# Landmark attention stage of a six-stage decoder kernel: four separate turns rewritten as one list of steps, and one small triangular inverse moved to VectorE

## The chip, the cores and the metric

One core of a Trainium2 chip runs one program. The metric is the device time of that program in microseconds (us), where the result holds for one launch over all four batches.

## What is computed

Two decoder layers with a LayerNorm behind each residual: delta rule, Mamba-like scan, sign FFN, landmark attention, cross attention, ternary FFN, on x of 4 x 512 x 512 in float32. The change is in the fourth (landmark) and has one small part in the first (delta).

```python
q, k, v = split(x @ w_qkv + b_qkv)                    # 32 heads of 16
q, k = rope(q), rope(k)                               # pairs of channels rotated by position
out_local = masked_softmax(q kT / 4, causal) v        # in blocks of 64 tokens
lmf = pool(k, v)                                      # softmax(pool_q k) v: 4 landmarks a block, 32 in all
lmf += attention(lmf @ w_lm_qkv) @ w_lm_out + b       # landmark to landmark
lmf += softmax((lmf @ w_l2t_q + b) k) v @ w_l2t_out + b   # landmarks read their tokens
gk, gv = split(lmf @ w_lm_kv + b)
out_global = masked_softmax(q gkT / 4, earlier blocks) gv
gate = sigmoid(x @ w_gate + b_gate)
y = ((1 - gate) * out_local + gate * out_global) @ w_out + b_out
```

In the delta stage the inverse of a unit lower triangular 32 x 32 matrix is needed for each chunk of 32 tokens and head; the kernel takes half a batch's heads at a time (eight such pairs, n = 0 to 7): 128 matrices stand side by side, one a partition, and are inverted in 31 columns.

## The kernel before

The program is a chain of stages (`STAGES`), each of which waits until the one before has stored all of its output. Each engine has its own instruction list. A stage with `unrolled` has one list over all four batches; the landmark stage has not: each engine runs a loop of four turns, one per batch (`sp_turn`, `pool_turn`, `pe_turn`, `act_turn`, `dve_turn`). PSUM's eight banks are a ring (`Ring`): each product has its place in the plan, and TensorE waits until the bank's former content is read.

A turn has these parts.

- **Front.** x is turned over on TensorE (L204) and copied by ScalarE (L213), the gate is projected (L237), then v, and for each of four token tiles q and k (L224, one projection is four float32 matmuls of 512 columns, and each float32 matmul is two records in the trace). VectorE adds the bias and rotates q and k token by token (L2478 to L2488), TensorE turns them over (L2212), ScalarE copies them to QT and KT (L2307). v is copied by 16 small DMAs into the zero-padded VV (L2034).
- **Local.** 16 items (channel chunk c, token tile t). GpSimd multiplies a block of KT with a head mask into Kz (L2049, two buffers, `landmark_kz`), TensorE makes the scores (L2234), VectorE adds the mask (L2575), takes the maximum (L2383), subtracts it (L2385), ScalarE takes exp (L2346), VectorE sums (L2495), TensorE transposes (L2241), ScalarE copies (L2351), TensorE multiplies with VV (L2252), ScalarE copies the result (L2355). The order is in `local_order`: scores of item i+2, transposes of i, values of i-1. Into each step one step of the landmark chain (`CHAIN`, 15 steps: pool, landmark attention, reading, global keys and values) is put. The normalization is left to the end: GpSimd multiplies the four output tiles with (1 - gate)/sum (L2055).
- **Global.** Eight items (token tile, half of the heads) with the landmarks' keys: scores (L2264), mask, maximum, subtract (L2634, L2383, L2385), exp, sum (L2605), transposes (L2271), values (L2278, token-major), then `mix`: scale by gate/sum and add to the local part (L2612 to L2624).
- **Out.** The mixed output is turned over (L2286), multiplied with w_out (L224), residual and bias are added (L2648, L2650), and the tiles are normalized and stored.

The stage's matrices (12 of 512 x 512 float32, 1 MB each) are loaded once at its begin and stay.

In the delta stage GpSimd does all eight inverses (L535 to L547, `pool_all`): a copy of the identity, and for each of 31 columns a product (L541) and a subtraction (L543), each waiting for the one before. SyncE cuts the matrices out through DRAM (L496, L500) and brings the inverse back through DRAM (L511, L515, `sp_inverse`); TensorE's triangles of that pair (L622, `pe_triangles`) wait for it. PSUM's ring has six banks there; VectorE's reads of V (L996, `dve_beta_v`) and of PT (L1005) release them.

Of the kernel before, what the change touches and what calls it, by code (L numbers as in the profile page):

```python
# [342 lines left out]
class Delta(Stage):  # L343
# [561 lines left out]

    def dve_all(self, dve):
        s = self
        for p in range(-1, s.PAIRS + 1):
# [972 lines left out]
class Landmark(Stage):  # L1881
# [3 lines left out]
    name, pool_works = "landmark", True  # L1885
# [4 lines left out]
    EPS = 1e-9  # L1890

    CHAIN_BANKS = {
        "pool_s": [(("pool", "s"), "dve")], "pool_T": [(("pool", "T"), "act")],
        "pool_v": [(("pool", 0), "dve"), (("pool", 1), "dve")],
        "lqk": [(("lq", "rows"), "dve"), ("lq", "dve"), (("lk", "rows"), "dve"), ("lk", "dve")], "lv": [("lv", "dve")],
        "ls": [(("ls", 0), "dve"), (("ls", 1), "dve")], "lpT": [("lpT", "act")], "lo": [("lo", "dve")],
        "loT": [("loT", "act")], "lout": [(("lout", "rows"), "dve"), ("lout", "dve")], "l2q": [(("l2q", "rows"), "dve"), ("l2q", "dve")],
        "read_s": [(("read", "s"), "dve")], "read_T": [(("read", "T"), "act")],
        "read_v": [(("read", 0), "dve"), (("read", 1), "dve")],
        "rout": [(("rout", "rows"), "dve"), ("rout", "dve")], "gkv": [(("gk", "rows"), "dve"), ("gk", "dve"), ("gv", "dve")],  # L1900
    }
    CHAIN = list(CHAIN_BANKS)
    SMALL = ["lq", "lk", "lout", "l2q", "rout", "gk"]

    def __init__(self, io, carve, ps, x_in, x_out):
        s = self
        s.io, s.x_in, s.x_out = io, x_in, x_out
        s.wqkv, s.wlm = carve(C, 3 * D), carve(C, 3 * D)
        s.wlo, s.wl2q, s.wl2o, s.wkv, s.wo = carve(C, D), carve(C, D), carve(C, D), carve(C, 2 * D), carve(C, D)
        s.wg = carve(C, s.H)  # L1910
        s.bqkv, s.blv, s.bgv, s.bo, s.bg = carve(3 * D), carve(D), carve(D), carve(D), carve(s.H)
        s.blq, s.blk, s.blo, s.bl2q, s.bl2o, s.bgk = (carve(C) for _ in range(6))
# [4 lines left out]
        s.rope = carve(T, 6, 8)  # L1917

        tokens, turned, rotated = carve(T, D), carve(C, L), carve(T, D)
        s.x, s.xT, s.xr = tokens, turned, rotated  # L1920
        s.raw, s.rot = rotated[:, 0:2], rotated[:, 2:4]
        s.Kz = Arena(tokens.rearrange("p t n -> p (t n)"))(2, s.HC, P)
        a = Arena(turned.rearrange("p t n -> p (t n)"))
        s.kz, s.vz, s.lm4 = a(C, s.HC, s.NL), a(s.HC, 4, s.DH), a(C, 4, s.NL)
        a = Arena(rotated.rearrange("p t n -> p (t n)"))
        s.lp, s.l2z = a(2, D), a(C, s.NB, s.HC, s.M)

        s.cs, s.cT, s.cmx, s.rows = carve(2, D), carve(4, P), carve(s.H), carve(2, P)
        s.tmp = s.cT.rearrange("p a n -> p (a n)")
        s.v, s.QT, s.KT, s.lout = carve(T, D), carve(C, L), carve(C, L), carve(T, D)  # L1930
        s.VV = carve(s.NB, C, 2, s.S)
        s.sc, s.p, s.pT = carve(2, D), carve(2, D), carve(2, 4, P)
        s.gate, s.ungated, s.lsum, s.gsum = (carve(T, s.H) for _ in range(4))
        s.mx = carve(2, s.H)
# [3 lines left out]
        s.r, s.y = s.v, s.QT  # L1938

        s.items = [(c, t) for c in range(C) for t in range(T)]  # L1940
        plan = [(("xT", t), "act") for t in range(T)]
        plan += [("gateT", "dve"), (("v", 0), "dve"), ("gate", "dve")] + [(("v", t), "dve") for t in range(1, T)]
        for t in range(T):
            plan += [(("q", t), "dve"), (("k", t), "dve")]
            if t:
                plan += [(("qT", t - 1), "act"), (("kT", t - 1), "act")]
        plan += [(("qT", T - 1), "act"), (("kT", T - 1), "act")]
        for what, i in s.local_order():
            if what == "landmarks":
                plan += s.CHAIN_BANKS[i]  # L1950
            else:
                plan += [((what, i), {"s": "dve", "t": "act", "o": "act"}[what])]
        for what, i in s.global_order():
            plan += [((what, i), {"gs": "dve", "gt": "act", "go": "dve"}[what])]
        plan += [(("oT", t), "act") for t in range(T)] + [(("y", t), "dve") for t in range(T)]
        s.ring = Ring("landmark", ps, 0, 8, plan)

    def local_order(self):

        n, step = len(self.items), 0
        for i in range(-2, n + 1):
            if i + 2 < n:
                yield "s", i + 2
            if 0 <= i < n:
                yield "t", i
            if 0 <= i - 1 < n:
                yield "o", i - 1
            if i >= -1 and step < len(self.CHAIN):  # L1970
                yield "landmarks", self.CHAIN[step]
                step += 1

    def global_order(self):

        n = 2 * T
        for i in range(-2, n + 1):
            if i + 2 < n:
                yield "gs", i + 2
            if 0 <= i < n:  # L1980
                yield "gt", i
            if i > 0 and i % 2 == 0:
                yield "go", i // 2 - 1

    def sp_before(self, sp):
        s, io, w = self, self.io, "landmark_weights"
        sp.e.dma_start(s.ident, io["c_masks"][:, 0, :]).then_inc(*sp.up(w, 16))
        for dst, src in ((s.blq, "D_blq"), (s.blk, "D_blk"), (s.blo, "D_blo"), (s.bl2q, "D_bl2q"),
                         (s.bl2o, "D_bl2o"), (s.bgk, "D_bgk"), (s.pool, "D_pool")):
            sp.e.dma_start(dst, io[src]).then_inc(*sp.up(w, 16))  # L1990
        for dst, src in ((s.bm16, "c_group16"), (s.gm32, "c_group32"), (s.m_local, "c_local"),
                         (s.m_gl, "c_global"), (s.valid, "c_valid0"), (s.rope, "c_rope")):
            sp.e.dma_start(dst, io[src]).then_inc(*sp.up(w, 16))
        sp.e.dma_start(s.m_lm[:s.NL], io["c_landmark"]).then_inc(*sp.up(w, 16))
        for dst, src in ((s.bg, io["D_bg"]), (s.bqkv, io["D_bqkv"])):
            sp.e.dma_start(dst, src.partition_broadcast(P)).then_inc(*sp.up(w, 16))
# [16 lines left out]
    def act_before(self, act):  # L2013
        act.e.wait_ge(*act.at_all("landmark_weights"))
# [1631 lines left out]
```

## Time and profile before

| | us |
|---|---|
| median of three runs | 3797.43 (3789.03 to 3804.51) |
| the profiled execution: its time | 3791.86 |
| its span, first to last instruction | 3790.1 |
| TensorE busy | 2899.1 (76%) |
| VectorE busy | 2316.3 (61%) |
| ScalarE busy | 1230.9 (32%) |
| GpSimd busy | 1104.9 (29%) |

Times in the trace count from the span's start. The landmark stage takes 1931.4 to 2855.6. A busy TensorE is not one at its peak: its records overlap, and the granted clock (1.00 is 2.4 GHz, 0.50 is 1.2 GHz) differs between stretches. Idle time of an engine that nobody waits for costs nothing.

### The profile page before, as it was taken

How to read it: one execution, taken by the hardware profiler on the slowest of the kernel's cores; microseconds unless marked ns; L12 is line 12 of the kernel's file. 1: busy time of each engine (PE TensorE's matmuls, PEld its weight loads, DVE VectorE, ACT ScalarE, POOL GpSimd, SP SyncE). 2: the span in 40 equal slices, each digit the busy share in tenths (PEclk: the TensorE clock that was granted, in tenths of full speed). 3: DMA queues.
4: the chain of work that ended last, by engine and by line, in shares of the span. 5: the costliest groups of instructions: out<-in, count | busy, mean ns of one | idle time of the engine just before them, and what ended most of it. 6: DMA issues, size and time to landing. Idle time of an engine off the chain costs nothing.

```text
span 3790.1 us, 53260 instructions
## 1 busy us (share of the span) xinstructions
PE 2899.1 (76%) x20710; PEld 1511.5 (40%) x20710; DVE 2316.3 (61%) x3434; ACT 1230.9 (32%) x2016; POOL 1104.9 (29%) x1044
## 2 busy tenths in 40 slices
PE   6688888755555655599968787888874798989877
PEld 4565655522121212244434545455452233333233
DVE  1233333338898989687728668585763565656577
ACT  3232323214434333111102212121221464645645
POOL 4433333325454645200003012020203442433000
PEclk8788998867777778899988888888876899999999
DMA  2212121112212020400050000000004543434211
GB/s 76 67 45 66 45 66 45 43 42 106 81 37 89 22 90 11 173 23 38 27 202 1 24 23 24 23 13 29 6 12 117 104 108 71 105 73 87 82 45 45
DMA packets 194861, 226.12 MB, mean 60 GB/s; under 512 B 98520, under 2 KB 130808, under 8 KB 193712
## 3 DMA queue, kind: packets, MB, share of 16 engines
q1 hardware_dynamic: 193520, 218.44, 20.5%
q0 software_dynamic: 1088, 4.19, 0.3%
q8 instruction: 172, 2.82, 0.3%
q14 instruction: 81, 0.66, 0.1%
HBM read 154.69 MB, written 54.92 MB: 55 GB/s over the span
## 4 chain that ended last, share of the span: by engine, by line
PE 38%; DVE 12%; issue 6%; ACT 3%; DMA 2%; POOL 1%; SPq 1%; DVEq 0%; ACTq 0%; POOLq 0%
PE ps L224 6%; PE ps L1723 4%; PE ps L1734 4%; PE ps L3001 3%; PE ps L2988 3%; PE ps L2976 2%; PE ps L2937 2%; PE ps L2967 2%; DVE arena L2383 1%; PE ps L2234 1%; PE ps L2278 1%; PE ps L2099 1%; DVE arena L1333 1%; PE ps L2252 1%; ACT arena L3079 1%
## 5 line engine op out<-in xcount | busy, mean ns | idle before, releaser
L3174 DVE TENSOR_REDUCE arena<-ps 128x1 f32<-128x512 f32 x512 | 330.4, 685 | 272.4 <-PE ps L2976 271.1
L224 PE MATMUL ps<-arena 128*128 128x512 f32 (+3 forms) x1296 | 469.6, 519 | 10.5 <-ACT arena L855 3.3
L1381 PE MATMUL ps<-arena 128*128 128x512 f32 x512 | 312.5, 755 | 130.0 <-POOL arena L1365 130.0
L1365 POOL TENSOR_TENSOR arena<-arena 128x1024 f32<-128x1024 f32 x128 | 309.5, 2418 | 298.7 <-DVE arena L1357 297.7
L3079 ACT ACTIVATE arena<-ps 128x512 f32<-128x512 f32 x512 | 288.0, 597 | 289.1 <-PE ps L2988 285.5
L1357 DVE TENSOR_TENSOR_SCAN arena<-ps,arena 128x1024 f32<-128x1024 f32 x128 | 291.6, 2278 | 63.6 <-ACT ps L1348 63.2
L2049 POOL TENSOR_TENSOR arena<-arena 128x1024 f32<-128x1024 f32 x64 | 127.7, 1999 | 598.0 <-ACT arena L2307 354.8
L224 PEld LDWEIGHTS ps<-arena 128*128 128x128 f32 (+2 forms) x1296 | 196.1, 155 | 250.6 <-issue 182.8
L541 POOL TENSOR_TENSOR arena<-arena 128x31 f32<-128x31 f32 (+15 forms) x248 | 150.0, 605 | 368.9 <-DMA arena<-d_a 350.1
L1348 ACT ACTIVATE ps<-arena 128x511 f32<-128x511 f32 x256 | 165.2, 680 | 241.2 <-DVE arena L1357 241.0
L1381 PEld LDWEIGHTS ps<-arena 128*128 128x128 f32 x512 | 114.8, 238 | 320.0 <-POOL arena L1365 190.0
L2988 PE MATMUL ps<-arena 99*128 99x512 bf16 x512 | 198.2, 390 | 55.1 <-ACT arena L3079 33.4
L2976 PE MATMUL ps<-arena 96*128 96x512 bf16 x512 | 197.9, 389 | 24.4 <-issue 18.9
L1723 PE MATMUL ps<-arena 128*128 128x512 bf16 x768 | 169.0, 382 | 8.0 <-issue 8.0
L1734 PE MATMUL ps<-arena 128*128 128x512 bf16 x768 | 166.9, 379 | 0.0
L1333 DVE TENSOR_TENSOR arena<-ps,arena 128x1024 f32<-128x1024 f32 x128 | 154.3, 1206 | 0.8
L1029 DVE TENSOR_TENSOR arena<-ps,arena 128x256 f32<-128x256 f32 x120 | 50.9, 425 | 158.9 <-PE ps L742 158.9
L3001 PE MATMUL ps<-arena 128*32 128x512 f32 x1024 | 141.6, 626 | 1.0 <-ACT arena L3079 1.0
L543 POOL TENSOR_TENSOR arena<-arena 128x31 f32<-128x31 f32 (+15 forms) x248 | 134.5, 542 | 19.4
L2874 POOL TENSOR_TENSOR arena<-arena 128x512 f32<-128x512 f32 x32 | 40.8, 1275 | 318.0 <-ACT arena L3052 318.0
L2988 PEld LDWEIGHTS ps<-arena 99*128 99x128 bf16 x512 | 49.7, 98 | 207.1 <-ACT arena L3079 143.1
L1377 PE MATMUL ps<-arena 128*128 128x512 f32 x32 | 32.3, 1111 | 116.1 <-DVE arena L1407 116.1
(337 smaller groups left out, 5394.9 us busy)
## 6 DMA issues: line engine op xcount, KB each, us to landing
arena<-d_bc SPq DMA_DIRECT2D x32, 1024.0 KB, 5.2
arena<-d_x SPq DMA_DIRECT2D x24, 1024.0 KB, 5.5
arena<-d_parts SPq DMA_DIRECT2D x192, 128.0 KB, 4.3
d_x<-arena SPq DMA_DIRECT2D x20, 1024.0 KB, 4.4
d_parts<-arena SPq DMA_DIRECT2D x32, 384.0 KB, 2.4
arena<-arena SPq DMA_DIRECT2D x64, 128.0 KB, 2.0
d_w<-arena SPq DMA_DIRECT2D x3, 1408.0 KB, 4.8
arena<-d_w SPq DMA_DIRECT2D x3, 1408.0 KB, 10.5
```

The costliest lines, as they stand in the source:

```text
L224: ins = pe.e.matmul(ps[:m, :n], lhsT(k), rhs(k), start=(k == 0), stop=(k == chunks - 1))
L1333: dve.e.tensor_tensor(s.h[:, i % s.HS].rearrange("p (w l) -> p w l", w=s.W), spread(s.ps[:, s.DTU, :], 1, s.W), s.bc[:, turn % s.SLOTS, 0] ...
L1357: dve.e.tensor_tensor_scan(h, s.dA[:, i % 2].rearrange("p w l -> p (w l)"), h, 0.0, ALU.mult, ALU.add).then_inc(*dve.up("scan_scanned"))
L1365: pool.e.tensor_tensor(h, h, s.bc[:, turn % s.SLOTS, 1], ALU.mult).then_inc(*pool.up("scan_hC"))
L1381: ins = pe.e.matmul(y, s.ident, s.h[:, i % s.HS, w * L:(w + 1) * L], start=False, stop=last)
L1723: ins = e.matmul(ps, s.up[:, k, m * P:(m + 1) * P], s.xp[i][:, k, :], start=(k == i == 0), stop=(k == C - 1 and i == 2))
L1734: ins = e.matmul(ps, s.hp[i][:, m, t * P:(t + 1) * P], s.down[:, m, :], start=(m == i == 0), stop=(m == s.FC - 1 and i == 2))
L2976: pe.e.matmul(s.rmax.bank((u, m)), s.Qs[:s.N, slot, h, t * P:(t + 1) * P], s.Ks[:s.N, slot, h, :], start=True, stop=True).then_inc(*s.rmax ...
L2988: pe.e.matmul(s.rexp.bank((u, i)), s.Ks[:s.N + 3, slot, s.G * g + j, k * P:(k + 1) * P], s.Qs[:s.N + 3, slot, s.G * g + j, :], start=True, ...
L3001: ins = e.matmul(ps[32 * j:32 * j + 32, :], s.V[:, u % s.SLOTS, k, s.G * g + j, :], s.E[:, k % 2, j, :], start=(k == 0), stop=(k == s.KEYS ...
L3079: act.e.activation(s.E[:, k % 2, j], s.rexp.bank((u, i)), ACT.Exp).then_inc(*s.rexp.empty(act, (u, i)))
L3174: dve.e.tensor_reduce(s.mx[:, u % 2, t, h:h + 1], s.rmax.bank((u, m)), AX.X, ALU.max, negate=True).then_inc(*s.rmax.empty(dve, (u, m)))
```

## The change

**Landmark.** The stage becomes `unrolled`: `schedule` yields one list of steps, and each engine walks it and does its share of each step. A batch is 20 local steps (k = -2 to 17), 11 global steps (k = -2 to 8) and 4 out steps. The front of batch b+1 is put into the steps of batch b: x, gate and v into local steps 0 to 7, and eight projections "r" (q and k of each of four channel chunks, already channel-major, so that they need not be turned over) into local steps 9, 10, 12, 13 and global steps -1, 1, 3, 5. Batch 0's front stands alone at the begin.

The rotation is now channel-major on GpSimd: ScalarE adds the bias on its copy from PSUM, two DMAs of SyncE's queue swap even and odd partitions, and GpSimd does three 128 x 512 operations.

```diff
+    def pool_rope(self, pool, b, r):
+        pool.e.wait_ge(*s.ring.at_emptied(pool, ("r", b, r)))
+        e.tensor_tensor(s.m1, s.raw[:, j % 2], s.cos, ALU.mult).then_inc(*pool.up("landmark_cos"))
...
+        pool.e.wait_ge(*pool.on("landmark_swapped", j))
+        e.tensor_tensor(s.sw[:, j % 2], s.sw[:, j % 2], s.sin, ALU.mult).then_inc(*pool.up("landmark_sin"))
...
+        e.tensor_tensor((s.QT, s.KT)[w][:, b % 2, c], s.m1, s.sw[:, j % 2], ALU.add).then_inc(*pool.up("landmark_rot"))
+    def sp_swap(self, sp, b, r):
+        sp.e.wait_ge(*s.ring.at_emptied(sp, ("r", b, r)))
...
+        for odd in range(2):
+            sp.e.dma_start(s.sw[odd::2, j % 2], s.raw[1 - odd::2, j % 2])
+        sp.e.wait_ge(*sp.on("landmark_swapped", j))
```

The softmax weights of the local and global items are normalized and gated before they are transposed, item by item: VectorE makes the factor, GpSimd multiplies. GpSimd's order in a local and a global step is this:

```diff
+            if phase == "local":
+                if s.item(k + 1) is not None:
+                    s.pool_scale(pool, b, k + 1)
+                if k == -2:
+                    s.pool_kz(pool, b, 0)
+                if s.item(k + 3) is not None:
+                    s.pool_kz(pool, b, k + 3)
+            if phase == "global" and s.item(k + 1, s.NG) is not None:
+                s.pool_g_scale(pool, b, k + 1)
+            for what, i in front:
+                if what == "r":
+                    s.pool_rope(pool, b + 1, i)
...
+            if phase == "global" and k >= s.NG - 3 and b + 1 < B:
+                for i in range(2):
+                    s.pool_pairs(pool, b + 1, 2 * (k - s.NG + 3) + i)
```

The other engines' order in a local step:

```diff
+    def pe_all(self, pe):
+            if phase == "local":
+                if s.item(k + 2) is not None:
+                    s.pe_scores(pe, b, k + 2)
+                if s.item(k) is not None:
+                    pe.e.wait_ge(*pe.on("landmark_scaled", b * s.N + k))
+                    s.pe_turn(pe, ("t", b, k), k)
+                if s.item(k - 1) is not None:
+                    s.pe_values(pe, b, k - 1)
...
+            if chain:
+                s.pe_landmarks(pe, chain, b)
+            for what, i in front:
+                s.pe_front(pe, what, b + 1, i)
+    def dve_all(self, dve):
+                if s.item(k + 2) is not None:
+                    s.dve_scores(dve, b, k + 2)
+                if s.item(k + 1) is not None:
+                    s.dve_factor(dve, b, k + 1)
+    def dve_factor(self, dve, b, i):
+        e.tensor_reduce(ls, s.p[:, i % 3].rearrange("p (h n) -> p h n", n=s.S), AX.X, ALU.add).then_inc(*dve.up_step(st))
...
+        e.scalar_tensor_tensor(ls, ls, s.EPS, s.rungated[:, b % 2, t, c * s.HC:(c + 1) * s.HC], ALU.max, ALU.mult).then_inc(*dve.up_step(st))
+        e.reciprocal(ls, ls).then_inc(*dve.up("landmark_factor"))
```

The value products come out channel-major: four local items fill one bank "o", and the global values are four products of 512 columns ("go", two at step 4 and two at step 8) added to it, so that the turning over before w_out (L2286), `mix` and GpSimd's scaling of the output (L2055) go. VV is now filled by four DMAs and eight GpSimd multiplications with a pair mask (`pool_pairs`). The bias b_out is added to x by GpSimd (local step 7), where VectorE did it before (L2650). The chain has 18 steps (lq, lk and gk, gv apart). Only w_q, w_k and w_gate stay; the ten matrices of the chain, v and w_out go through three slots of 1 MB and are loaded anew for each batch (`sp_matrix`).

**Delta.** GpSimd's loop begins at n = 1; the first inverse is done on VectorE by the same operations, put behind `dve_beta_k` of pair 0:

```diff
-        for n in range(s.PAIRS):
-            if n:
-                pool.e.wait_ge(*pool.on("delta_t32_out", n - 1))
+        for n in range(1, s.PAIRS):
+            pool.e.wait_ge(*pool.on("delta_t32_out", n - 1))
...
                     if i == 1:
                         s.dve_beta_k(dve, n)
+                        if n == 0:
+                            s.dve_inverse(dve)
```

## Rows read from the trace of the kernel before

**Rows 1.** Busy time by stretch: the stage's begin and one turn

```profile
1931.40:1954.60 23.20, 0.00 (x0) 0.00 (x0) 0.81 (x4) 0.00 (x0) 4.37 (x2) 0.50 0.78 287
...
2181.67:2404.80 223.13, 183.67 (x1591) 113.00 (x1595) 152.98 (x249) 48.69 (x93) 37.24 (x21) 0.84 0.07 21
```

Columns of rows 1 and 2: stretch, us; busy us (instructions) of TensorE, its weight loads, VectorE, ScalarE, GpSimd; granted clock; DMA share; GB/s.

**Rows 2.** The same view, one turn in its four parts

```profile
2181.67:2236.00 54.33, 48.49 (x161) 23.57 (x161) 30.05 (x46) 5.52 (x9) 3.78 (x2) 0.94 0.14 39
2236.00:2338.00 102.00, 84.32 (x1199) 53.09 (x1198) 80.28 (x126) 26.25 (x55) 28.16 (x14) 0.83 0.04 12
2338.00:2378.00 40.00, 28.30 (x146) 23.61 (x145) 30.26 (x53) 9.82 (x18) 5.29 (x5) 0.76 0.08 27
2378.00:2404.80 26.80, 22.56 (x90) 12.73 (x93) 12.40 (x25) 7.11 (x11) 0.00 (x0) 0.82 0.02 6
```

**Rows 3.** Groups by line in the turn 2181.67 to 2404.80

```profile
L2049 POOL TENSOR_TENSOR arena<-arena 128x1024 f32<-128x1024 f32 x16 | 31.9, 2002 | 158.7 <-ACT arena L2307 98.3 <-PE ps L2234 60.4
...
L2385 DVE TENSOR_TENSOR arena<-arena 128x512 f32<-128x512 f32 (+1 forms) x25 | 21.6, 864 | 0.9
L2383 DVE TENSOR_REDUCE arena<-arena 128x8 f32<-128x512 f32 (+2 forms) x25 | 17.7, 707 | 0.9
...
L2398 DVE RECIPROCAL arena<-arena 128x8 f32<-128x8 f32 x2 | 0.4, 203 | 0.1
```

**Rows 4.** GpSimd's scaling of a 128 x 512 tile: one line's instructions, ns min/median/max

```profile
L2055 POOL TENSOR_TENSOR arena<-arena x16: 1055/1058/1507, 2115.9 to 2789.7; 128x512 f32<-128x512 f32 x16
```

**Rows 5.** Timeline of the turn, TensorE: start, us, engine, line

```profile
2240.49 1.08 PE L2234 MATMUL ps<-arena 128*64 128x512 f32 x4
...
2241.50 0.66 PE L2241 MATMUL ps<-arena 128*128 128x128 f32 x4
...
2248.28 1.98 PE L2234 MATMUL ps<-arena 128*64 128x512 f32 x4
...
2260.05 0.91 PE L2252 MATMUL ps<-arena 128*64 128x32 f32 x16
```

**Rows 6.** Timeline, TensorE: seven projections, 56 records

```profile
2187.72 24.20 PE L224 MATMUL ps<-arena 128*128 128x512 f32 x56
```

**Rows 7.** Groups by line in the same turn: two steps of the chain

```profile
L2099 PE MATMUL ps<-arena 64*32 64x32 f32 (+1 forms) x488 | 9.2, 236 | 0.7 <-issue 0.7
...
L2143 PE MATMUL ps<-arena 32*128 32x32 f32 x16 | 3.6, 397 | 2.9 <-ACT arena L2324 2.9
```

**Rows 8.** The cross stage's like rotation: GpSimd's product, the swap's landing

```profile
L2874 POOL TENSOR_TENSOR arena<-arena x32: 1264/1276/1287, 2890.1 to 3470.1; 128x512 f32<-128x512 f32 x32
...
L2796 SPq DMA_DIRECT2D arena<-arena x64: 465/568/601, 2890.0 to 3468.4; - x64
...
DMA to landing us min/median/max: 1.9/2.0/5.5
```

**Rows 9.** Timeline: VectorE alone, and beside a GpSimd operation

```profile
2203.57 0.43 DVE L2486 TENSOR_TENSOR arena<-arena 128x256 f32<-128x256 f32 x1
...
2213.57 1.89 POOL L2049 TENSOR_TENSOR arena<-arena 128x1024 f32<-128x1024 f32 x1 [92.42 <-ACT arena L2307]
2213.59 2.16 DVE L2486 TENSOR_TENSOR arena<-arena 128x256 f32<-128x256 f32 x1
```

**Rows 10.** Timeline: from the turn's last product to its store

```profile
2398.19 0.69 DVE L2648 TENSOR_TENSOR arena<-arena,ps 128x512 f32<-128x512 f32 x1 [1.29 <-PE ps L224]
...
2403.54 0.40 SPq L311 DMA_DIRECT2D d_x<-arena  x1
```

**Rows 11.** Timeline of the delta stage's begin

```profile
60.03 0.26 POOL L541 TENSOR_TENSOR arena<-arena 128x31 f32<-128x31 f32 x1 [45.68 <-DMA arena<-d_a]
...
72.30 8.61 PE L605 MATMUL ps<-arena 128*128 128x256 f32 x32
...
101.64 0.27 POOL L543 TENSOR_TENSOR arena<-arena 128x31 f32<-128x31 f32 x1
...
110.14 3.21 PE L622 MATMUL ps<-arena 128*32 128x128 f32 x64 [29.24 <-DMA arena<-d_t]
```

More of the change, by code:

```diff
@@ L1881 @@
 class Landmark(Stage):
-    name, pool_works = "landmark", True
+    name, pool_works, unrolled = "landmark", True, True
     H, DH, M, S = 32, 16, 4, 64
@@ L1890 @@
     EPS = 1e-9
[L1892 to L1901, printed above, removed]
@@ L1937, in __init__ @@
         s.norm = Norm("landmark", carve)
[L1938 to L1983, printed above, removed]
+        s.steps = list(s.schedule())
+        s.ring = Ring("landmark", ps, 0, 7, [e for step in s.steps for e in s.entries(*step)])
+        s.ro = Ring("landmark_o", ps, 7, 1, [(("o", b, c), "act") for b in range(B) for c in range(C)])
@@ new lines, in __init__, with turns, schedule @@
+        s.uses = [(name, b, n) for n, step in enumerate(s.steps) for name, b in s.matrices(*step)]
+        s.use = {use[:2]: i for i, use in enumerate(s.uses)}
+    def turns(self, name):
+        s = self
+        if name in s.ONCE + s.RING:
+            return 1
+        return B * s.N if name in s.BY_ITEM else B * s.NG if name in s.BY_GLOBAL else B * len(s.TURNED) if name in s.BY_TURNED else B
+    def schedule(self):
+        s = self
+        nothing = {}
+        for fronts in (s.LOCAL_FRONT, s.GLOBAL_FRONT):
+            for k in fronts:
+                yield "front", -1, k, None, fronts[k]
+        for b in range(B):
+            more = b + 1 < B
+            for k in range(-2, s.N + 2):
+                yield "local", b, k, s.CHAIN[k + 1] if 0 <= k + 1 < len(s.CHAIN) else None, (s.LOCAL_FRONT if more else nothing).get(k, [])
+            for k in range(-2, s.NG + 1):
+                yield "global", b, k, None, (s.GLOBAL_FRONT if more else nothing).get(k, [])
+            for t in range(T):
+                yield "out", b, t, None, []
@@ L1994, in sp_before @@
[L1994 to L2002 removed]
+        s.loaded = 0
@@ new lines, in act_sqrt, with act_all @@
+    def act_sqrt(self, act, b):
+        act.b = b
+        self.norm.act_sqrt(act)
+        act.b = 0
+    def act_all(self, act):
+        s = self
+        for phase, b, k, chain, front in s.steps:
+            if phase == "local":
+                if k == -2 and b:
+                    s.act_sqrt(act, b - 1)
+                if s.item(k) is not None:
+                    s.act_turned(act, b, k)
+                if k >= 1 and (k - 1) % T == T - 1:
+                    s.act_out(act, b, (k - 1) // T)
+            if phase == "global":
+                s.act_global(act, b, k)
+            if chain:
+                s.act_landmarks(act, chain, b)
+            for what, i in front:
+                s.act_front(act, what, b + 1, i)
+            if phase == "local" and s.item(k + 2) is not None:
+                s.act_exp(act, b, k + 2)
+        s.act_sqrt(act, B - 1)
@@ new lines, in dve_scale @@
+    def dve_scale(self, dve, b):
+        dve.b = b
+        self.norm.dve_scale(dve, self.x, self.x)
+        dve.b = 0
+    def dve_all(self, dve):
+        s = self
+        dve.e.wait_ge(*dve.at_all("landmark_late"))
+        for phase, b, k, chain, front in s.steps:
+            if phase == "local":
+                if k == -2 and b:
+                    s.dve_scale(dve, b - 1)
+                if s.item(k + 2) is not None:
+                    s.dve_scores(dve, b, k + 2)
+                if s.item(k + 1) is not None:
+                    s.dve_factor(dve, b, k + 1)
+            if phase == "global":
+                s.dve_global(dve, b, k)
+            if phase == "out":
+                s.dve_y(dve, b, k)
+            if chain in ("pool_T", "read_T"):
+                s.dve_pool_weights(dve, chain, b)
+            if chain:
+                s.dve_landmarks(dve, chain, b)
+            for what, i in front:
+                s.dve_front(dve, what, b + 1, i)
+            if chain in s.SMALL:
+                s.dve_small(dve, chain, b)
+        s.dve_scale(dve, B - 1)
```

1260 lines of the change are left out of this document (688 added, 572 removed).

## The prediction

> **What bounds the kernel now.** I read first the busy time by stretch. The landmark stage is a head of 23.2 us without matmuls and four like turns of 223.1 us, in which TensorE is busy for 184, VectorE for 153 and GpSimd for only 37 us [rows 1]. By parts, a turn spends 54.3 us on the front, 102.0 on local, 40.0 on global and 26.8 on the output [rows 2]; in none is one engine busy all the time, so each part is bound by the hand-overs between engines as well. What the change can save is therefore idle time, and what it costs is any new hand-over. The groups by line give the prices of the operations, the timeline those of TensorE's pieces and of the delta stage's begin. The profiled execution took 3791.86 us for a span of 3790.1, 5.6 below the median of 3797.43; differences found against it are added to the median. About 0.5%, 19 us, is what a measurement of this kernel can tell from no change.
>
> **Delta.** The inverse holds GpSimd from 60.0 to 101.9 us, and TensorE, idle for 29.2 us, gets it at 110.1, 8.2 us later [rows 11]. VectorE does 62 operations of 31 to 256 elements, 176 in the mean. It needs 0.20 us for 8 elements and 0.43 for 256 [rows 3, 9], so some 0.35 for 176, and 0.04 between dependent ones: 24 us for 41.9. The inverse would be at TensorE at 92.3. But VectorE's reads of V stand behind it in its queue (before: done by 59), the bank of V is wanted for PT, and TensorE's 8.6 us for K of the next pair [rows 11] come behind PT, in order. PT starts at 84.5, K at 89, the triangles at 97.5: late next is this queue, not the inverse. Gain 110.1 - 97.5 = **12.6 us**, between 0 (were the queue worse) and 18.
>
> **Landmark, what leaves.** VectorE loses the rotation, five operations for each of 8 tiles, by 0.43 alone and up to 2.16 beside GpSimd [rows 9] some 27 us a turn, and about 11 of mixing and bias, and gets 9 of factors: 153 becomes about 127 us. TensorE loses two turnings and the short value products. The new matmul time is below the old 184. Neither is a saving unless it is on the path; both stay well below 223.
>
> **What is new: one loop through four engines.** GpSimd's queue has, in each local step, the scaling of item i and behind it Kz of item i+2; Kz is what the scores of i+2 wait for, VectorE takes these scores before it makes the factor of i+1, and the next scaling waits for that factor. So one item takes one turn of this loop, however idle the engines are: scaling 1.06 [rows 4], Kz 1.90 [rows 9], scores 1.08 at full clock or 1.98 at half [rows 5], mask, maximum, subtract 3 x 0.69 + gaps = 2.15, sum and two tiny operations 0.69 + 0.2 + 0.2 + gaps = 1.13 [rows 3], and five hand-overs of about 0.05 to 0.13, together 0.3 (DVE to TensorE and back, from the gaps in the timeline, my estimate). That is 7.6 us; I take 7.7, as most steps are dense enough for the full clock. Before, scores and Kz were tied to no softmax, and the 102 us for 16 items came to 6.4 each [rows 2].
>
> **A batch, from the last product of the batch before (y3) on.**
> - y3 to the scores of item 2: norm until its store 5.3 [rows 10], two scorings, a factor, scaling, Kz, scores: 15.
> - Twelve loops to item 14: 12 x 7.7 = 92.4.
> - Steps in which TensorE is longer than the loop. A projection is 8 records, 24.2/56 x 8 = 3.46 us [rows 6]. Step 4 has lv and v: 1.1 + 0.66 + 0.91 [rows 5] + 6.9 = 9.6 and the gate; step 6 has 3.6 for lpT [rows 7] and v: 9.7; step 12 waits for the reading's weights, then has a q, 2.5 over. With VectorE's longer steps 1, 5, 7 and 10 some 9 together.
> - Item 14 to the first global scores: 36. Here the queue is the reading's values (about 4.2), the projection, the copy, the swap (second DMA 0.57 behind the first, 2.0 to land [rows 8]), GpSimd's two last products 1.27 each [rows 8], and only then the scaling of item 15, on which the transposes, and behind them gk and gv, wait.
> - Global: 13 to the transposes of item 1, then three loops of two items, each bound by projection 3.46, copy 0.7, swap 2.8, two products 2.6, scaling 1.06, transposes 0.66 and hand-overs = 11.7, hence 35; two pair products, transposes, copy, four value products 3.5, the add: 7; four output projections 13.8: 69 together.
>
> Sum 15 + 92 + 9 + 36 + 69 = 221; TensorE's idle stretches in the global loops bring half clock to some first matmuls, as the 0.76 there now shows [rows 2]: 3 more, **224 us a batch, against 223.1 now**, though a front of 54.3 is inside. The front is hidden, the loops cost as much.
>
> **Begin and end.** The matmuls can start after about 11 us instead of 23.2 [rows 1], since only 2 MB are waited for, not 3; x, gate and v take 20, then eight rotations follow at GpSimd's 3.9 us each (three products at 1.27 [rows 8]), with eight pair products of 1.06 [rows 4] and two Kz between: 80 us to the first scores. The first batch has no norm before it, 220. The last has no front: no long steps (9), no swap in the tail (10), a VectorE-bound global part (17): 188. Norm and store 10. Stage: 80 + 220 + 2 x 224 + 188 + 10 = 946, against 924.2: **+22 us**. The bounds of the dearest unknown, the loop, are 7.0 (hand-overs nothing, a scaling at the least) and 8.6 (half clock): 4 x 12 x -0.7 = -34, + 43. The reloading of matrices is 30 MB more, hidden: the DMA share of a turn is 0.07 [rows 1], and each slot is asked for two steps or more ahead; were that cover gone, each swap behind a load would wait some us, 8 times a batch.
>
> Forecast: 22 - 12.6 = +9, **3806 us**; its own range is 3765 to 3840.
>
> **Rivals.** *The loop does not decide (faster).* If GpSimd runs ahead, or the hand-overs overlap more than I think, TensorE and VectorE order the local part: before's turn less its front, 223.1 - 54.3 = 169, plus some 20 of the front's 48 busy us [rows 2] that find no gap, 189 a batch. Stage 80 + 186 + 2 x 189 + 175 + 10 = 829, -95, with delta 3690; half of it 3740. For it: GpSimd has 37 busy us of 223, all engines have room. Against: the order in GpSimd's queue. *The port (slower).* A VectorE operation of two SBUF inputs took 2.16 beside Kz and 0.43 alone [rows 9]; subtractions took 0.864 in the mean instead of 0.69 [rows 3]. GpSimd's work rises from 37 to 16 Kz (30) + 24 scalings (25) + 8 rotations (31) + pairs and bias (13) = 99 us a batch, 44% of the time, so that the chain's writes of masked keys and the subtractions meet it. With 50 such operations, 44% of them held for half of 1.3 us, 14 us; if it falls in the loop, and with the half clock in each second one, 236 to 240 a batch, 4 x 14 = +56: 3862. It decides from 0.5 us a step on.
>
> The Trainium skill ("SBUF — State Buffer", Who interferes with whom) says that an operation of VectorE with two SBUF inputs and a GpSimd one that reads SBUF exclude each other for the whole of the first, while one with a PSUM or a single input is left alone; by that rule the mask and the sums of the loop are safe, and only the subtraction and the chain's products pay, which gives this rival its 14 us and not more. The trace agrees in the one pair of rows 9.
>
> *Delta gains nothing*: +12.6 on any of these, within the ranges.
>
> **How the numbers follow.** The forecast 0.50 (of it faster by over 0.5% 0.07, within 0.25, slower 0.18), the loop that does not decide 0.27, the port 0.23. Faster 0.34, within 0.5% 0.25, slower 0.41. The range for 8 in 10 takes half of either rival: 3715 to 3870; cases of both signs hold most of the chance, so the forecast's own range stands above.
>
> **What would show it.** Right: local steps of 7.5 to 8 us with GpSimd's scaling and Kz back to back, then idle; TensorE's scores waiting for GpSimd in each; global steps of two at 11 to 12 us with a wait for the swap; starts of "y3" 220 to 228 apart; triangles of pair 0 at 97 us. Wrong: batches under 210 us, or scores that wait for VectorE or a bank; matmuls waiting for a matrix; inverse at TensorE above 105 us.

## The result, and the profile after

The kernel after takes 3861.34 us in the median (3852.47 to 3868.58); the kernel before, run beside it, 3793.23. The ratio is 1.0176, with a 95% interval of 1.0155 to 1.0196: **slower by 1.8%**. The forecast was 3806, its own range 3765 to 3840, the range for 8 in 10 went from 3715 to 3870. So the sign of the forecast and the wide range held; its own range missed by 21 us, and of the measured 68 us between the medians the forecast had 9.

The page's first part, of the kernel after: less TensorE and VectorE work than before, GpSimd 217 us busier, and the span 60.6 us longer than the 3790.1 of before.

```profile
span 3850.7 us, 50818 instructions
...
PE 2842.7 (74%) x20326; PEld 1416.5 (37%) x20326; DVE 2261.0 (59%) x3450; ACT 1227.1 (32%) x1955; POOL 1321.9 (34%) x1201
```

Busy time by stretch, kernel after, columns as in [rows 1]: the head up to the first scores, then each batch from its first scores to the next batch's, the last one to the end of its output products.

```profile
1918.50:2011.20 92.70, 46.90 (x145) 22.87 (x145) 6.18 (x14) 10.76 (x15) 42.59 (x35) 0.74 0.50 157
2011.20:2239.70 228.50, 167.65 (x1471) 88.16 (x1471) 130.67 (x224) 45.28 (x75) 103.69 (x77) 0.84 0.21 65
2239.70:2471.90 232.20, 164.10 (x1472) 87.31 (x1471) 133.97 (x237) 46.77 (x77) 102.61 (x76) 0.83 0.25 78
2471.90:2710.60 238.70, 170.34 (x1472) 90.36 (x1471) 135.44 (x237) 46.89 (x77) 102.37 (x76) 0.80 0.24 76
2710.60:2907.30 196.70, 131.56 (x1327) 72.63 (x1326) 123.01 (x229) 37.26 (x62) 57.46 (x42) 0.74 0.15 49
```

A turn of before was 223.1 [rows 1]. No engine is busy for three quarters of a batch, and the batch is still longer than the turn, which had its front in line. Forecast were 80 for the head and 220, 224, 224, 188 for the batches; measured are 92.7 and 228.5, 232.2, 238.7, 196.7. The stage begins at 1918.5 instead of 1931.4, and with its last store it takes about 998 us (last store issued at 2911.8, landed some 4 us later) instead of 924.2.

The loop, in the last batch, where no front lies beside it. Timelines of TensorE, VectorE and GpSimd, kernel after: start, us, engine, line, and in brackets the idle time before and what ended it.

```profile
2781.03 1.97 PE L2389 MATMUL ps<-arena 128*64 128x512 f32 x4 [2.94 <-POOL arena L2151]
...
2789.31 1.87 PE L2389 MATMUL ps<-arena 128*64 128x512 f32 x4 [3.06 <-POOL arena L2151]
...
2783.11 0.69 DVE L2765 TENSOR_TENSOR arena<-ps,arena 128x512 f32<-128x512 f32 x1 [1.73 <-PE ps L2389]
2783.84 0.69 DVE L2629 TENSOR_REDUCE arena<-arena 128x8 f32<-128x512 f32 x1
2784.56 0.69 DVE L2631 TENSOR_TENSOR arena<-arena 128x512 f32<-128x512 f32 x1
2785.17 0.68 DVE L2779 TENSOR_REDUCE arena<-arena 128x8 f32<-128x512 f32 x1
2785.88 0.17 DVE L2783 SCALAR_TENSOR_TENSOR arena<-arena 128x8 f32<-128x8 f32 x1
2786.08 0.20 DVE L2785 RECIPROCAL arena<-arena 128x8 f32<-128x8 f32 x1
...
2786.36 1.04 POOL L2158 TENSOR_TENSOR arena<-arena 128x512 f32<-128x512 f32 x1 [5.38 <-DVE arena L2785]
2787.36 1.90 POOL L2151 TENSOR_TENSOR arena<-arena 128x1024 f32<-128x1024 f32 x1
```

Read in a ring: scores 2781.03 to 2783.0, mask to factor 2783.11 to 2786.28, scaling at 2786.36, Kz at 2787.36, the next scores at 2789.31. That is 8.28 us, and every start follows the end before it within 0.11 us. The twelve loops of this batch (scores of item 2 at 2723.43, of item 14 at 2822.40) take 99.0, 8.25 each.

### The profile page after: what moved, and what is told of

Its sections match the earlier page's. It is cut to its first block and busy times, and to the rows that moved or that the text cites. A ratio compares the mean times of both kernels' runs of the same rounds, so it can differ in the third digit from the quotient of the medians.

```text
span 3850.7 us, 50818 instructions
## 1 busy us (share of the span) xinstructions
PE 2842.7 (74%) x20326; PEld 1416.5 (37%) x20326; DVE 2261.0 (59%) x3450; ACT 1227.1 (32%) x1955; POOL 1321.9 (34%) x1201
## 5 line engine op out<-in xcount | busy, mean ns | idle before, releaser
L224 PE MATMUL ps<-arena 128*128 128x512 f32 (+3 forms) x1296 | 496.5, 540 | 10.2 <-ACT arena L854 3.4
L1384 POOL TENSOR_TENSOR arena<-arena 128x1024 f32<-128x1024 f32 x128 | 309.6, 2419 | 298.9 <-DVE arena L1376 297.9
L1400 PE MATMUL ps<-arena 128*128 128x512 f32 x512 | 312.1, 754 | 130.4 <-POOL arena L1384 130.4
L540 POOL TENSOR_TENSOR arena<-arena 128x31 f32<-128x31 f32 (+15 forms) x217 | 130.5, 601 | 319.6 <-DMA arena<-d_a 303.2
L2389 PE MATMUL ps<-arena 128*64 128x512 f32 x256 | 91.6, 808 | 134.5 <-POOL arena L2151 134.5
L2158 POOL TENSOR_TENSOR arena<-arena 128x512 f32<-128x512 f32 x64 | 66.8, 1043 | 304.7 <-DVE arena L2785 304.7
L2397 PE MATMUL ps<-arena 128*128 128x128 f32 x384 | 82.0, 351 | 96.2 <-POOL arena L2164 83.5
L3084 POOL TENSOR_TENSOR arena<-arena 128x512 f32<-128x512 f32 x32 | 40.8, 1274 | 316.8 <-ACT arena L3262 316.8
L2765 DVE TENSOR_TENSOR arena<-ps,arena 128x512 f32<-128x512 f32 x64 | 43.9, 685 | 166.5 <-PE ps L2389 166.0
```

The source lines that it names most:

```text
L224: ins = pe.e.matmul(ps[:m, :n], lhsT(k), rhs(k), start=(k == 0), stop=(k == chunks - 1))
L1384: pool.e.tensor_tensor(h, h, s.bc[:, turn % s.SLOTS, 1], ALU.mult).then_inc(*pool.up("scan_hC"))
L1400: ins = pe.e.matmul(y, s.ident, s.h[:, i % s.HS, w * L:(w + 1) * L], start=False, stop=last)
```

## The experiments

All are compared with runs of the kernel before on the same chip. "After" is 1.0176; 0.001 of ratio is 3.8 us. A distance to the kernel after is the difference of two such ratios, each with an interval of some 0.002 to either side, so it is good to about 11 us.

**1. Delta's part alone.** The kernel before, with `dve_inverse` called for pair 0 and `pool_all` beginning at pair 1.

> The kernel before with delta's part of the change alone: pair 0's inverse on VectorE, nothing of the landmark stage touched. My theory of a separate gain: delta's stage ends 12.6 us earlier and no later stage gives it back, so the kernel runs 0.3% faster than before, near 3781 us. Rival: the freed time is given back in a later stage (GpSimd's pair 1 inverse or the next stage's loads), within 4 us of the kernel before. If the first holds, the landmark part of the change alone cost about 80 us.

Measured: 0.9962 (0.9948 to 0.9977), 14 us faster. Delta's part pays, as forecast; by this run the rest of the change then costs 1.0176 / 0.9962 = 1.0215, some 81 us by the medians and 74 by the two profiled stages. Timelines of TensorE and, below, VectorE in the kernel after:

```profile
88.20 3.64 PE L673 MATMUL ps<-arena 128*32 128x128 f32 x64 [20.87 <-DVE arena L1015]
91.77 7.74 PE L604 MATMUL ps<-arena 128*128 128x256 f32 x32
99.43 1.96 PE L621 MATMUL ps<-arena 128*32 128x128 f32 x64
...
60.49 0.21 DVE L915 TENSOR_TENSOR arena<-arena 128x31 f32<-128x31 f32 x1 [7.12 <-DMA arena<-d_a]
...
87.25 0.21 DVE L917 TENSOR_TENSOR arena<-arena 128x31 f32<-128x31 f32 x1
87.37 1.28 DVE L1015 TENSOR_TENSOR arena<-ps,arena 128x512 f32<-128x512 f32 x2
```

The inverse takes 27.0 us (60.49 to 87.46) instead of 41.9. What the triangles wait for now is the queue behind it: VectorE's read of V (L1015), PT (L673), K (L604), then the triangles (L621) at 99.4 instead of 110.1 [rows 11]. They also take 1.96 us instead of 3.21, so that they end 12.0 earlier, about the 12.9 by which the landmark stage begins earlier.

**2. Kz before the scaling.** In `pool_all`, local steps, GpSimd first writes Kz of item k+3 and then scales item k+1:

```diff
-                if s.item(k + 1) is not None:
-                    s.pool_scale(pool, b, k + 1)
                 if k == -2:
                     s.pool_kz(pool, b, 0)
                 if s.item(k + 3) is not None:
                     s.pool_kz(pool, b, k + 3)
+                if s.item(k + 1) is not None:
+                    s.pool_scale(pool, b, k + 1)
```

> The kernel after, with one edit: in each local step GpSimd writes Kz of item k+3 before it scales the weights of item k+1. Nothing is added or removed. Theory (the loop factor, scaling, Kz, scores, mask to subtract, factor decides): the loop is cut, so the twelve loops of the last batch, 99.0 us now (8.25 each), fall to what TensorE's and VectorE's own queues need, 5.5 to 6.5 each or 66 to 78 us, and the batches with a front fall by 10 to 25 us each: 3765 to 3815 us in all, near 3790. Rival (the port that VectorE and GpSimd share decides, or the clock of TensorE): the same GpSimd work lies beside VectorE and the same matmuls run, so less than 10 us is won and the time stays at 3850 to 3865.

Measured: 1.0049 (1.0029 to 1.0069), 48 us faster than the kernel after, with not one operation less. TensorE and, below, GpSimd, last batch, kernel of experiment 2 (line numbers as in the kernel after):

```profile
2719.65 1.08 PE L2389 MATMUL ps<-arena 128*64 128x512 f32 x4
...
2724.42 1.08 PE L2389 MATMUL ps<-arena 128*64 128x512 f32 x4
...
2730.00 1.08 PE L2389 MATMUL ps<-arena 128*64 128x512 f32 x4
...
2720.25 1.90 POOL L2151 TENSOR_TENSOR arena<-arena 128x1024 f32<-128x1024 f32 x1
2724.03 1.04 POOL L2158 TENSOR_TENSOR arena<-arena 128x512 f32<-128x512 f32 x1 [1.88 <-DVE arena L2785]
```

Scores are 4.8 to 5.6 us apart here and wait for nothing of GpSimd; Kz is ready ahead. Over the whole stage TensorE's wait for Kz falls from 134.5 to 51.4 us (groups by line: instructions, busy, mean ns, idle before and its releaser), first the kernel after, then experiment 2:

```profile
L2389 PE MATMUL ps<-arena 128*64 128x512 f32 x256 | 91.6, 808 | 134.5 <-POOL arena L2151 134.5
```

```profile
L2389 PE MATMUL ps<-arena 128*64 128x512 f32 x256 | 80.2, 714 | 51.4 <-POOL arena L2151 51.4
```

Part of this wait moves on: before the local transposes TensorE now waits 51.6 us for the scaling, which is no longer first in GpSimd's queue, where it waited 12.7. From item 3 to 14 a step is 6.5 (71.5 / 11) instead of 8.2. The total is in the expected range; two parts of the expectation were not met. The twelve loops of the last batch took 86.8, not 66 to 78: 15.3 of it is the step from item 2 to 3, since the scores of item 2 now come only 3.1 behind the first ones, and steps in which TensorE waits for the landmark chain are still 8 to 10 us. And two of the three batches with a front lost less than 10 us (219.9, 225.3, 223.4; 8.6, 6.9 and 15.3 below the kernel after); the last batch gave 19.5.

**3. Kz twice.** `pool_kz` writes its tile, waits for the write, and writes it again.

> The kernel after with each local Kz written twice by GpSimd (64 more multiplies of 1.9 us). Theory of the loop through GpSimd: nearly each of the 1.9 us is on the path, 14 or 15 times a batch, and the time rises by 100 to 120 us, to 3960 to 3985. Rival (TensorE's or VectorE's own queue decides and GpSimd only seems late): the rise is under 50 us.

Measured: 1.0500 (1.0476 to 1.0524), by the ratios 123 us slower than the kernel after; by the medians (3967.27 and 3861.34) it is 106, and by the stage in the two profiled executions (1105 and 998) 107. TensorE, two scores of the last batch in that kernel:

```profile
2896.97 1.97 PE L2391 MATMUL ps<-arena 128*64 128x512 f32 x4 [5.12 <-POOL arena L2153]
...
2907.17 1.98 PE L2391 MATMUL ps<-arena 128*64 128x512 f32 x4 [4.14 <-POOL arena L2153]
```

10.20 us apart instead of 8.28, 1.9 more: one Kz in such a loop, at its full price. The twelve loops took 21 to 24 us more in batches 1 to 3, of the 23 that twelve times 1.95 would make. Over the stage 64 times 1.95 is 125, so 107 of it, or all by the ratios, is on the path: the loop runs through GpSimd in most steps of every batch.

**4. The rotation cut in two.**

```diff
         e.tensor_tensor(s.m1, s.raw[:, j % 2], s.cos, ALU.mult)...
+    def pool_rope_rest(self, pool, b, r):
         pool.e.wait_ge(*pool.on("landmark_swapped", j))
         ...
+            for turned in late:
+                s.pool_rope_rest(pool, *turned)
+            late = []
             for what, i in front:
                 if what == "r":
                     s.pool_rope(pool, b + 1, i)
+                    late.append((b + 1, i))
```

The wait for the swapped rows and the two products behind it come one step later, behind that step's scaling (batches 1 to 3).

> The kernel after with GpSimd's rotation cut in two in batches 1 to 3: the multiply by the cosine stays in its step, and the wait for the swapped rows, the multiply by the sine and the add come one step later, behind that step's scaling. The same operations run. Theory (the wait of GpSimd for SyncE's swap, 2.6 us and in the global steps up to 9.2 us with the projection, holds the scaling behind it): each of the four global loops of a batch falls from about 13.7 to 9 to 11 us, 10 to 18 us a batch and 30 to 55 us in all, so 3805 to 3830 us. Rival (the half-clock projections of 5.4 to 5.8 us in TensorE's queue set these loops): under 8 us, 3853 to 3861.

Measured: 1.0082 (1.0058 to 1.0107), 36 us faster. From the scores of item 14 to the next batch's first scores: 117.9, 118.0, 120.3 in the kernel after, 104.3, 105.7, 106.9 here; the last batch, without a rotation, is unchanged (196.7 and 197.9). A wait in the middle of GpSimd's queue, for a copy by SyncE, held the scalings behind it for 13 us a batch.

**5. Both.**

> The kernel after with both edits: Kz of item k+3 before the scaling of item k+1, and the rotation cut in two. The first edit alone moved the ratio to the kernel before by -0.0127, the second by -0.0094. Theory: they cut two different loops (local and global), so the gains add, a ratio of 0.994 to 0.998, some 3770 to 3782 us, the first of these kernels below the kernel before. Rival: both free the same time of GpSimd, and one gain takes in most of the other: 1.001 to 1.005.

Measured: 0.9941 (0.9920 to 0.9962). The sum of the two edits, 1.0176 - 0.0127 - 0.0094 = 0.9955, lies inside. They cut two different loops, and the rival's 1.001 to 1.005 is out. With both, the stage takes 903.6 us to the end of its last products and, with the 9 us behind them, some 913, where it took 924.2 before.

**6. Extra matmuls in TensorE's idle time.** Before the wait for Kz in local steps without a front, and before the wait for the scaling in global steps:

```diff
+    def pe_extra(self, pe, ps, b):
+        for _ in range(2):
+            for b2 in range(2):
+                pe.e.matmul(ps[64 * b2:64 * b2 + 64], self.QT[:, b % 2, 0, :64], self.KT[:, b % 2, 0, :], start=True, stop=True)
```

> The kernel after with work added and none taken away: in each local step without a front, while TensorE waits for Kz, and in each global step before it waits for the scaling, it runs two more pairs of score matmuls whose result is overwritten (about 2.2 us at the full clock, 3.9 at half). Theory of the clock: TensorE's idle time in the loop is why its scores take 1.98 us instead of 1.08 and the projections of the global steps 5.4 to 6.5 instead of 3.6; kept at work it stays at 2.4 GHz and, with more work, the kernel is 15 to 40 us faster, 3820 to 3845. Rival: the clock costs little on the path, or the extra matmuls lie in the way of the scores: no gain or a loss, 3855 to 3900.

Measured: 1.0184 (1.0159 to 1.0210), no difference that shows, where 15 to 40 us had been expected. TensorE, last batch of that kernel:

```profile
2810.34 1.08 PE L2396 MATMUL ps<-arena 128*64 128x512 f32 x4 [0.67 <-POOL arena L2151]
...
2815.11 1.94 PE L2384 MATMUL ps<-arena 128*64 128x512 f32 x8
2817.85 1.08 PE L2396 MATMUL ps<-arena 128*64 128x512 f32 x4 [0.81 <-POOL arena L2151]
```

Here a loop is 7.51 us: scores at 1.08, the full clock, and the extra pairs (L2384) still inside the wait. The granted clock of the last batch rose from 0.73 to 0.89 (stretch 2710 to 2900 in both). But the twelve loops took 96.9, not the 90 of twelve such loops: where the extra pairs began late they stood in front of the scores (step from item 2 to 3: 11.4 instead of 8.7), and from item 14 to the next batch it was 118 to 120, as before.

**7. Extra matmuls only in the long waits.**

> The kernel after with the extra matmuls again, now only in TensorE's long waits: two pairs before the scores in local steps from the third on that have neither a front nor the turning of a softmax, six pairs before the global transposes of items 3, 5 and 7 in batches 0 to 2 (waits of 7.8 to 9.2 us). In the run with extras everywhere, bare loops of the last batch took 7.3 to 7.5 us instead of 8.25 with the scores at 1.08 instead of 1.98, but the extras before every global item stood in the way. Theory (half clock is what the loops of the kernel after have over the sum of their terms): some 16 bare loops fall by 0.9 and the nine global loops by 1.5 to 2.5 each, 15 to 35 us in all, 3825 to 3845 (a ratio of 1.009 to 1.014). Rival (no clock on the path): 1.016 to 1.019.

Measured: 1.0185 (1.0164 to 1.0205), a miss for the theory as it was priced; the rival's 1.016 to 1.019 held. Bare steps of the last batch fell to 7.35 to 7.5 again, others rose to 10.5, and twelve took 97.2. Before the transposes of item 5 there was no long wait in the kernel after (1.56 us), so six pairs stood in the way; from item 14 to the next batch it was 122 to 123. What the half clock costs over the whole path was so not measured. In a single bare loop it is 0.7 to 0.9 us (8.25 against 7.35 to 7.5), and filling TensorE's idle time gave nothing back in the total.

**8. The masking products of the values moved.** On top of both edits; GpSimd's eight `pool_pairs` a batch go from global steps 5 to 8 to the four out steps, in batch 0 behind the first two Kz, with the four copies that feed them issued after the swaps.

> The kernel with both edits, and besides GpSimd's eight multiplies that mask the doubled values (9.8 us a batch) moved: in batches 1 to 3 from the last global steps to the steps of the output projection, in batch 0 behind the rotations and the first two Kz, with the copies that feed them issued after the swaps. Theory: two multiplies stand in front of each of the last scalings (4.0 us of TensorE's wait before the last global transposes) and all eight in front of batch 0's rotations: 8 to 15 us for the head and 3 to 5 for each of three ends, 17 to 28 us below the kernel with both edits, near 3755. Rival: GpSimd had this time free, under 5 us.

Measured: 0.9901 (0.9875 to 0.9927), 15 us below both edits, a little under the expected 17 to 28. Up to the first scores the head became shorter by more than that: they came 74.0 us after the stage's begin instead of 94.6 in experiment 5. GpSimd in this kernel, the first rotation's second product:

```profile
1958.24 1.27 POOL L2180 TENSOR_TENSOR arena<-arena 128x512 f32<-128x512 f32 x1 [1.32 <-DMA arena<-arena]
```

It waits 1.3 us for its swap, where it waited 12.5 in experiment 5: 11.2 us are the copies that no longer stand before the swap, 9.8 the eight products. The products now stand before the Kz of item 2 and wait 4.3 us for their copies, so that to the scores of item 2 it was 91.8 us instead of 100.0 (8 won). Batches 1 and 2 took 208.2 instead of 211.6 (3.4 won, as expected).

**9. All rotations in the local steps.** On top of that.

> The same, and besides all eight turned projections and rotations of the next batch in local steps 8 to 15, none in the global steps. Theory: a global loop with a projection (5 to 6.5 us of TensorE) is 3 to 5 us longer than one without, so the global part of batches 0 to 2 falls by 12 to 18 us; eight local steps take 3.8 us more of GpSimd each, 6.8 us in all, which is about what they last, so they give back 0 to 10 us: 5 to 40 us below the run before it, near 3735. Rival: the local steps now go by GpSimd's own queue, 8 us or more each, and it is no faster, or up to 15 us slower.

Measured: 0.9894 (0.9868 to 0.9919). The two intervals lie over one another: in the time it is undecided. The traces of the two show both sides of the exchange. From a batch's first global scores to the next batch it was 57.6, 60.4 and 56.9 us instead of 66.3, 66.3 and 66.6, 24 less in sum, where 12 to 18 had been expected: projections and rotations did cost the global steps 8 us a batch. The steps before it took 2.7, 4.3 and 6.3 more, 13 in sum, where 0 to 10 had been expected. What is left is 11 us of the stage in these two executions; the ratios show 3, within their noise. This and the run before are the fastest of the case, 1% faster than the kernel before and 2.8% than the kernel after.

**10. GpSimd kept busy beside VectorE.** The kernel after, and behind Kz in the local steps 0 to 7 and all of the last batch's:

```diff
+                        for _ in range(3):
+                            pool.e.tensor_tensor(s.m1, s.cos, s.sin, ALU.mult)...
+                            pool.e.wait_ge(*pool.at_step("landmark"))
```

> The kernel after with three more multiplies of 1.27 us on GpSimd behind Kz, in the local steps 0 to 7 and in all of the last batch's, where GpSimd waits 4 to 5 us for the next factor; their result is not used. They end before the factor, so they lengthen no queue, but they lie beside VectorE's mask, maximum and subtract. Theory of the port as a price that the kernel after nearly escapes: the subtraction rises from 0.69 to about 1.6 us and a tiny operation may be held too, 0.9 to 1.6 us in each of some 38 steps, 35 to 60 us, 3895 to 3920. Rival (VectorE beside GpSimd costs nothing in the loop): within 8 us of the kernel after, 3853 to 3869.

Measured: 1.0283 (1.0265 to 1.0301), 40 us slower than the kernel after, in the expected range; twelve loops of the last batch took 108.6 instead of 99.0. The total is as the theory had it, but not its place. First, the added multiplies do not end before the factor everywhere, as the expectation had it. GpSimd in the step of the last batch that also adds b_out to x (L2223):

```profile
2825.16 3.96 POOL L2207 TENSOR_TENSOR arena<-arena 128x512 f32<-128x512 f32 x3
2829.20 5.25 POOL L2223 TENSOR_TENSOR arena<-arena 128x512 f32<-128x512 f32 x4
2834.42 1.03 POOL L2158 TENSOR_TENSOR arena<-arena 128x512 f32<-128x512 f32 x1
```

The scaling (L2158) waits for nothing there but GpSimd's own queue, and the step takes 12.1 us instead of 8.6, in each of the four batches: 14 of the 40 us are a longer queue and no matter of the port. Second, groups by line, landmark stage, the subtraction: kernel after, then experiments 10 and 5.

```profile
L2631 DVE TENSOR_TENSOR arena<-arena 128x512 f32<-128x512 f32 (+1 forms) x100 | 79.7, 797 | 3.5
```

```profile
L2636 DVE TENSOR_TENSOR arena<-arena 128x512 f32<-128x512 f32 (+1 forms) x100 | 85.2, 852 | 3.5
```

```profile
L2642 DVE TENSOR_TENSOR arena<-arena 128x512 f32<-128x512 f32 (+1 forms) x100 | 97.2, 972 | 3.5
```

Subtractions rose by 5.5 us only; the products for the landmarks' keys rose by 9.7, the factor's tiny operation with two inputs by 5.0, and the added multiplies themselves took 1.37 us instead of 1.27. How much of the other 26 us each of these made was not settled. In experiment 5 the subtractions take 17.5 us more than in the kernel after, and that kernel is 89 us faster. So VectorE and GpSimd do hold each other up, but this is not what the two edits won back.

## What the prediction had right, and where its sizes were off

The sign is right, but +9 us lies inside the 19 that the prediction itself called no change, and slower had a chance of 0.41 in it; the form of the loops is what held, the size did not. Its own range does not follow from its own bounds either: -34 and +43 about 3806 make 3772 to 3849, it says 3765 to 3840. Both miss the measured time.

*Delta, gain 12.6.* Right: 14 measured, by the interval 9 to 20; the landmark stage begins 12.9 us earlier, the triangles came at 99.4 where 97.5 was forecast, and behind the queue that was named. The inverse took 27.0 us for 24.

*One loop through four engines.* Right, and shown by cutting it (experiment 2) and by lengthening it (experiment 3). *The size, 7.7.* The sum was right for the clock that it took: 7.3 to 7.5 was measured where the scores took 1.08. The step that failed is "as most steps are dense enough for the full clock": in the last batch, without a front, the scores took 1.97 in most loops, which makes 8.25, +6.6 us for twelve. In the batches with a front the twelve loops and their long steps took 100.3, 101.4 and 105.7, where 92.4 + 9 = 101.4 was forecast (the 105.7 has one step of 11.3).

*Item 14 to y3, 36 + 69 = 105.* Here most of the error is: 118 to 120, so 13 to 15 us a batch (in batch 1: 5.0 before the first global scores, 1.1 to the transposes of item 1, 6.3 in the three loops of two items, 41.3 for 35, and 0.8 behind them); against it stand the 3 counted for the clock and a batch's begin, 12.8 for 15. The form was right (swap, products and scaling in one queue), and each global loop of two items, forecast at 11.7, had something more in it. The step that failed is this term: it took the projection at the full clock and the swap with nothing before it in its queue. TensorE and GpSimd, batch 1, kernel after:

```profile
2409.05 0.66 PE L2397 MATMUL ps<-arena 128*128 128x128 f32 x4 [2.49 <-POOL arena L2164]
...
2423.12 1.11 PE L2397 MATMUL ps<-arena 128*128 128x128 f32 x4 [7.81 <-POOL arena L2164]
2424.03 5.40 PE L224 MATMUL ps<-arena 128*128 128x512 f32 x8
...
2436.59 0.66 PE L2397 MATMUL ps<-arena 128*128 128x128 f32 x4 [1.56 <-POOL arena L2164]
...
2418.62 1.77 POOL L2177 TENSOR_TENSOR arena<-arena 128x512 f32<-128x512 f32 x1 [3.40 <-DMA arena<-arena]
2420.53 1.53 POOL L2182 TENSOR_TENSOR arena<-arena 128x512 f32<-128x512 f32 x1
2422.03 2.05 POOL L2164 TENSOR_TENSOR arena<-arena 128x512 f32<-128x512 f32 x2
...
2446.76 2.48 POOL L2192 TENSOR_TENSOR arena<-arena 128x512 f32<-128x512 f32 x2
```

```profile
2404.60 5.88 SPq L2091 DMA_DIRECT2D arena<-arena  x4
2413.89 28.68 SPq L2101 DMA_DIRECT2D arena<-arena  x6
```

The first (2409.05 to 2423.12, 14.07) has a swap that came 4.7 us after its issue instead of 2.8, behind four copies of v (L2091, not in the sum), and products of 1.77 and 1.53 instead of 1.27. The second (13.47) has the projection at 5.40 instead of 3.46, at a granted clock of 0.67, between the two levels. The third (13.72) has two masking products, 2.48, in front of the scaling, which the sum had only behind the loops. That these extra terms are the cause is read off this trace; of them the masking products were tried (experiment 8: 3.4 a batch), the queueing of the swap's wait in experiment 4. Between item 14 and the first global scores the projections of this batch took 4.57, 5.40 and 5.75 at granted clocks of 0.64 to 0.79; at 3.46 each they would be 5.3 shorter together, about what this part is over (41.0 for 36).

*Head, 80.* Measured 92.7, 13 more. "Eight rotations follow": they could not. GpSimd, kernel after:

```profile
1954.84 1.26 POOL L2175 TENSOR_TENSOR arena<-arena 128x512 f32<-128x512 f32 x1 [35.26 <-ACT arena L2498]
1968.54 1.27 POOL L2177 TENSOR_TENSOR arena<-arena 128x512 f32<-128x512 f32 x1 [12.43 <-DMA arena<-arena]
```

The first swap stood in SyncE's queue behind the issue of the copies of v (5.97 us) and of a matrix (2.10): it was issued at 1959.43, 4.6 us after the first product began, and its rows landed 9.1 us after that instead of 2.6, so that GpSimd waited 12.4. Experiment 8, with the copies behind the swaps, takes 11.2 of this wait away. The prediction counted GpSimd's queue here and not SyncE's.

*Last batch, 188.* 196.7: 6.6 of the 8.7 are the half-clock loops above. *Sum.* Head 13, batches 40, end -1: 52 us more than the forecast's +22, which gives the measured +74.

*Rival "the loop does not decide".* False for this kernel: the bare scores wait for Kz (134.5 us in the stage). In the kernel of experiment 2 the bare scores shown no longer wait for it. *Rival "the port".* Its 3862 is the measured time and its 236 to 240 a batch near the measured 228 to 239, but for another reason: in the loop shown above no operation is held. Elsewhere some are. Over the stage the 96 subtractions of 128 x 512 take 0.76 in the mean for 0.69 alone, the 64 and 32 factor operations 0.25 and 0.38 for 0.17, and four operations of 32 x 32 1.90 for 0.17; that is some 26 us (an estimate from these groups), and how much of it is on the path was not measured. The rival counted 56. It took the half clock in each second loop as well, and that part was real.

The rule of the Trainium skill ("SBUF — State Buffer", Who interferes with whom) was read too narrowly in the prediction: it also counts the factor's small operation with two SBUF inputs (0.17 alone, up to 0.91 in the kernel after), and it names copies and operations with a scalar among those that can take the shared ports. The trace agrees with that as well (below).

## What to carry to other kernels

When two works stand in one engine's queue, ask of the first which wait it carries and of the second who waits for it: here a scaling that waits for a softmax stood in front of a product that the next scores wait for, and exchanging two lines took 48 us (give or take 11) off without removing an instruction. Likewise a wait for a DMA in the middle of a queue should be parted from the work before it, so that what can run runs ahead. A sum of such a loop must be made at the clock that the loop's own idle time leaves, and must count each copy that stands in front of a short one in SyncE's queue.

## What was not expected of the hardware

Tiny operations of VectorE can last as long as the GpSimd operation that they meet. Timelines of GpSimd and VectorE, kernel after:

```profile
2779.09 1.90 POOL L2151 TENSOR_TENSOR arena<-arena 128x1024 f32<-128x1024 f32 x1
...
2777.92 1.16 DVE L2745 TENSOR_REDUCE arena<-arena 32x32 f32<-32x1024 f32 x1
2779.11 1.90 DVE L2747 TENSOR_SCALAR arena<-arena 32x32 f32<-32x32 f32 x1
```

An operation of 32 x 32 with one input took 1.90 us, begun 0.02 after Kz; in experiment 10, begun 0.04 us before Kz, it took 0.17, and Kz 1.89, no longer than elsewhere. So the small one was held where it began second; that a GpSimd operation is held in turn this pair does not show. In all four batches of the kernel after it took 1.90, in all four of experiment 10 0.17. Extra matmuls lifted the granted clock of the last batch from 0.73 to 0.89 and made single loops 0.7 to 0.9 us shorter, the kernel not.
